# Q, K and V of two blocks at a time, and the second block's input ahead of the weights

## The chip, the cores and the metric

The kernel runs on the 8 cores of one Trainium2 chip, each core on one batch item of its own with nothing exchanged. The metric is the device time in microseconds (us) of the slowest core.

## The reference, cut to what matters

```python
def _L0_attn_ref(x, W_qkv, b_qkv, W_out, b_out):       # x: (8, 4096, 1024)
    qkv = x @ W_qkv + b_qkv
    q, k, v = jnp.split(qkv, 3, axis=-1)
    scores = jnp.einsum('bqd,bkd->bqk', q, k) / 32
    attn = jax.nn.softmax(scores, axis=-1)
    return jnp.einsum('bqk,bkd->bqd', attn, v) @ W_out + b_out

x = _layernorm(x + _L0_attn_ref(x, ...))
x = _layernorm(x + _L0_ffn_ref(x, controller, f1, f2, bias))   # 64 experts, arg-max routing in groups of 16 tokens
```

Only the first line of it, the projections to Q, K and V, is touched by the change.

## The kernel before, in words

Each core has x (4096 x 1024) and its transpose in float32. The program is five phases, one behind the other: the projections; attention with the output projection and the first layer norm; the router; the experts; and the combination with the second layer norm. Every engine has its own list of instructions, written by hand in program order with semaphore waits between them; nothing reorders them. All matmuls are issued at lines 129 and 132 (129 is the last of an accumulation, which counts a semaphore up), all DMAs at line 118, most work of ScalarE and VectorE at line 139.

The first phase has three kinds of transfers.

- Casting copies, float32 to bfloat16, all issued by POOL (GpSimd) in one burst and carried by one queue, q0: the transposed x in four pieces (columns 0 to 512, 512 to 1024, 1024 to 2048, 2048 to 4096) from DRAM to a DRAM scratch tensor `xbft`, each by `emit_xpiece`; the weights in 24 pieces of 128 x 1024 (8 for each of Q, K and V) into the tile `arenaA`; and at the end the whole of x into the scratch tensor `xbf` for use in the second phase.
- Loads, issued by SP (SyncE, queue q1): for each block of 512 columns eight copies of 128 x 512 from `xbft` into one of two buffers in `arenaA`. A load waits for its piece of `xbft` and for the last matmul that read the buffer (`xblk_T`).
- Stores, issued by ScalarE (queue q10): Q doesn't stay in SBUF. Each 128 x 512 result of Q is written by an activation into one of two slots of the tile `qstage`, and from there to the scratch tensor `qsp`. The activation waits until the store before last, from the same slot, has landed.

The work goes over 8 blocks of 512 columns. For each block TensorE makes 8 results of Q, 8 of K and 8 of V, each of 8 matmuls of 512 columns into one of the eight PSUM banks `pb`. Q and K take turns on banks 0 to 3 and are evicted by ScalarE, K into the tile `arenaB`; V takes turns on banks 4 to 7 and is evicted by VectorE into `arenaC`. Before a bank is written again TensorE waits for its last eviction (`bank_free`). The buffer of block b is given back at the end of V of block b, in line 273:

```python
        xblk_T[buf] = P_cnt["sT"]
```

and is loaded for block b+2 while block b+1 is computed. Then the second phase begins with SP's load of Q from `qsp`.

Of the kernel before, what the change touches and what calls it, by code (L numbers as in the profile page):

```python
# [10 lines left out]
AF = mybir.ActivationFunctionType  # L11
# [3 lines left out]
NCH = 8  # L15
# [6 lines left out]
def build_nc(S=4096, debug_scratch=False, stop_phase=99):  # L22
# [4 lines left out]
    NB = S // 512  # L27
# [26 lines left out]
    qsp_d = nc.dram_tensor("qsp", [NCH, 128, S], BF16, kind=SCR).ap()  # L54
# [9 lines left out]
    A = sb("arenaA", [128, 32768], BF16)  # L64
    B = sb("arenaB", [128, max(S * NCH, ISG_END)], BF16)
    C_ = sb("arenaC", [128, max(NT * 1024, NT * 512 + S + 512 + NT * 64 + QC + 4096 + 64)], BF16)
    FP = sb("arenaF", [128, 2048], F32)
    QS = sb("qstage", [128, 1024], BF16)
    BQ = sb("s_bqkv_pc", [128, 16], F32)
# [9 lines left out]
    pb = [es_.enter_context(nc.psum_tensor(f"pb{i}", [128, 512], F32))  # L79
          for i in range(8)]  # L80

    XB0 = 24576
# [25 lines left out]
    P_cnt = {s: 0 for s in CHANNELS + ["sT", "sV", "sC"]}  # L108
# [6 lines left out]
    def dma(eng, chan, dst, src, **kw):  # L115
        P_cnt[chan] += 16
        op(eng, lambda e, d=dst, s=src, kw=kw, sm=chan:
           e.dma_start(d, s, **kw).then_inc(sems[sm], 16))  # L118
        return P_cnt[chan]

    def wait(eng, sname, v):
        if v and v > 0:
            op(eng, lambda e, sm=sname, vv=v: e.wait_ge(sems[sm], vv))

    def t_mm(out, lhsT, rhs, start, stop, inc=False):
        if inc:
            P_cnt["sT"] += 1
            op("tensor", lambda e, o=out, l=lhsT, r=rhs, st=start, sp=stop:
               e.matmul(o, l, r, start=st, stop=sp).then_inc(sems["sT"], 1))  # L129
        else:  # L130
            op("tensor", lambda e, o=out, l=lhsT, r=rhs, st=start, sp=stop:
               e.matmul(o, l, r, start=st, stop=sp))  # L132
        return P_cnt["sT"]
# [13 lines left out]
    def c_op(method, *args, inc=False, **kw):  # L147
        return eng_op("scalar", "sC", method, *args, inc=inc, **kw)
# [27 lines left out]
    def emit_xpiece(i):  # L176
        if i < len(xpieces):
            lo, hi, ch = xpieces[i]
            dma("gpsimd", ch, xbft_d[:, lo:hi], xt_d[:, lo:hi])

    emit_xpiece(0)
    for pi, (koff, pref) in enumerate(((0, "wc"), (1024, "wck"), (2048, "wcv"))):
        for k in range(NCH):
            dma("gpsimd", "%s%d" % (pref, k),
                A[:, k * 3072 + koff: k * 3072 + koff + 1024],
                wqkv_d[k * 128:(k + 1) * 128, koff:koff + 1024])
        emit_xpiece(pi + 1)
    xbc_done = dma("gpsimd", "xbc", xbf_d[:, :], x_d[:, :])
    dma("sync", "sm", BQ[:], bqkv_pc_d)
    dma("sync", "sm", GLM[:], glmask_d)  # L190
# [2 lines left out]
    sm_done = dma("sync", "sm", FP[:, 0:1024], bv_t_d)  # L193
# [5 lines left out]
    bank_free = [("sV", 0)] * 8  # L199
    xblk_T = [0, 0]  # L200

    for b in range(NB):
        buf = b % 2
        xoff = XB0 + buf * 4096
        xchan = "xa%d" % buf
        wait("sync", xq_chan(b), 16)
        wait("sync", "sT", xblk_T[buf])
        xv = 0
        for c in range(NCH):
            xv = dma("sync", xchan, A[:, xoff + c * 512: xoff + (c + 1) * 512],  # L210
                     xbft_d[c * 128:(c + 1) * 128, b * 512:(b + 1) * 512])

        wait("tensor", xchan, xv)

        for kind in ("Q", "K"):
            koff = 0 if kind == "Q" else 1024
            for m in range(NCH):
                pbi = m % 4
                sem, val = bank_free[pbi]
                wait("tensor", sem, val)  # L220
                tv = 0
                for k in range(NCH):
                    if b == 0 and m == 0:
                        wait("tensor",
                             ("wc%d" if kind == "Q" else "wck%d") % k, 16)
                    lhsT = A[:, k * 3072 + koff + m * 128:
                             k * 3072 + koff + m * 128 + 128]
                    rhs = A[:, xoff + k * 512: xoff + (k + 1) * 512]
                    tv = t_mm(pb[pbi][:], lhsT, rhs, k == 0, k == NCH - 1,
                              inc=(k == NCH - 1))  # L230
                wait("scalar", "sT", tv)
                wait("scalar", "sm", sm_done)
                if kind == "Q":
                    slot = m % 2
                    qchan = "qs%d" % slot
                    wait("scalar", qchan, P_cnt[qchan])
                    qsl = QS[:, slot * 512: slot * 512 + 512]
                    cv = c_op("activation", qsl, pb[pbi][:], AF.Identity,
                              inc=True, bias=BQ[:, m:m + 1])
                    wait("scalar", "sC", cv)  # L240
                    dma("scalar", qchan, qsp_d[m, :, b * 512:(b + 1) * 512], qsl)
                else:
                    cv = c_op("activation",
                              B[:, m * S + b * 512: m * S + (b + 1) * 512],
                              pb[pbi][:], AF.Identity, inc=True,
                              bias=BQ[:, 8 + m:8 + m + 1])
                bank_free[pbi] = ("sC", cv)

        wait("vector", "sV", init_v)
        wait("vector", "sm", sm_done)  # L250
        for sub in range(4):
            tt = b * 4 + sub
            for half in range(2):
                pbi = 4 + (sub * 2 + half) % 4
                sem, val = bank_free[pbi]
                wait("tensor", sem, val)
                tv = 0
                for k in range(NCH):
                    if b == 0 and sub == 0 and half == 0:
                        wait("tensor", "wcv%d" % k, 16)  # L260
                    lhsT = A[:, xoff + k * 512 + sub * 128:
                             xoff + k * 512 + sub * 128 + 128]
                    rhs = A[:, k * 3072 + 2048 + half * 512:
                            k * 3072 + 2048 + (half + 1) * 512]
                    tv = t_mm(pb[pbi][:], lhsT, rhs, k == 0, k == NCH - 1,
                              inc=(k == NCH - 1))
                wait("vector", "sT", tv)
                vv = v_op("tensor_tensor",
                          C_[:, tt * 1024 + half * 512: tt * 1024 + (half + 1) * 512],
                          pb[pbi][:], FP[:, half * 512:(half + 1) * 512],  # L270
                          ALU.add, inc=True)
                bank_free[pbi] = ("sV", vv)
        xblk_T[buf] = P_cnt["sT"]

    qkv_T_done = P_cnt["sT"]
    if stop_phase <= 1:
# [45 lines left out]
    for qt in range(NQ):  # L322
# [4 lines left out]
        for pbi in (0, 1, 7):  # L327
            sem, val = bank_free[pbi]
# [5 lines left out]
        for sub in range(2):  # L334
            tt = qt * 2 + sub
            slot = tt % 2
# [29 lines left out]
        for kt in range(NKT):  # L366
# [5 lines left out]
            else:  # L372
                wait("scalar", "sT", sc_T[kt])
                if kt >= 4:
                    wait("scalar", "sT", kt_T[kt - 4])
                exp_v[kt] = c_op("activation", ebuf, pb[sp][:, 0:256], AF.Exp,
                                 inc=True, scale=1.0 / 32.0, bias=SM[:, 0:1])
# [10 lines left out]
            for c in range(NCH):  # L388
                pbi = 2 + c // 2
# [4 lines left out]
                lhsT = C_[:, kt * 1024 + c * 128: kt * 1024 + c * 128 + 128]  # L394
# [20 lines left out]
        for c in range(NCH):  # L415
            pbi = 2 + c // 2
# [195 lines left out]
    for qc in range(4):  # L612
        q0 = qc * QC
        base = (qc % 2) * QC
        for nb in range(QC // LGW):
            pbi = 6 + nb % 2
            sem, val = bank_free[pbi]
            wait("tensor", sem, val)
            wait("tensor", "cb", cbf_done)
            tv = 0  # L620
            for k in range(NCH):
                lhsT = C_[:, CBF + k * 64: CBF + (k + 1) * 64]
                if k < 3:
                    if k == 0 and nb == 0:
                        wait("tensor", "ha%d" % qc, P_cnt["ha%d" % qc])
                    rhs = A[:, HFA + k * S + q0 + nb * LGW:
                            HFA + k * S + q0 + (nb + 1) * LGW]
                else:
                    if qc == 0 and nb == 0:
                        wait("tensor", hfch[k], hf_done[k])  # L630
                    rhs = B[:, k * S + q0 + nb * LGW: k * S + q0 + (nb + 1) * LGW]
                tv = t_mm(pb[pbi][0:64, 0:LGW], lhsT, rhs, k == 0, k == NCH - 1,
                          inc=(k == NCH - 1))
# [35 lines left out]
    for ec in range(4):  # L669
# [4 lines left out]
        for t in range(NT):  # L674
            slot = t % 4
# [6 lines left out]
            tv = 0  # L682
            for c in range(NCH):
                pbi = b0 + c // 4
                qtr = c % 4
                if qtr == 0:
                    sem, val = bank_free[pbi]
                    wait("tensor", sem, val)
                lhsT = ht4(slot)[:, c * 128:(c + 1) * 128]
                rhs = C_[:, PB + t * 512 + ec * 128: PB + t * 512 + (ec + 1) * 128]  # L690
                tv = t_mm(pb[pbi][:, qtr * 128:(qtr + 1) * 128], lhsT, rhs,
                          qtr == 0, qtr == 3, inc=(c == NCH - 1))
# [83 lines left out]
        for esl in range(16):  # L776
            es = ec * 16 + esl
            slot = esl % 4
            if esl + 3 < 16:
                load_fw(esl + 3)  # L780
            cv = cv_cur
# [5 lines left out]
            for g0 in range(0, G, 128):  # L787
# [3 lines left out]
                for pbj in pb_pair:  # L791
                    sem, val = bank_free[pbj]
                    wait("tensor", sem, val)
                tv = 0
                for half in range(2):
                    pbj = pb_pair[half]
                    lhsT = B[0:64, INB + slot * 256 + g0:
                             INB + slot * 256 + g0 + gw]
                    rhs = B[0:64, F2B + slot * 1024 + half * 512:
                            F2B + slot * 1024 + (half + 1) * 512]  # L800
                    tv = t_mm(pb[pbj][0:gw, :], lhsT, rhs, True, True,
                              inc=(half == 1))
# [96 lines left out]
    for t in range(NT):  # L899
        slot = t % 5  # L900
# [7 lines left out]
        for half in range(2):  # L908
            sem, val = bank_free[b0 + half]
# [93 lines left out]
```

## Time and profile before

| what | value |
|---|---|
| runs shown | 2490.02 and 2619.9 us, median 2554.96 |
| the profiled execution | 2497.26 us |
| its span on the slowest core (core 0) | 2495.7 us |
| spans of the eight cores | 2457.5 to 2495.7 us |
| mean granted TensorE clock of the cores | 0.837 to 0.851 |
| TensorE busy, core 0 | 1962.3 us, 79% of the span |
| ScalarE, VectorE, POOL busy | 554.7, 516.7, 128.9 us |

The span goes from the first to the last instruction of a core; the device time of the profiled execution is 1.6 us more. Busy times overlap, so they don't add up to the span. All rows below are of core 0.

### The profile page before, as it was taken

How to read it: one execution, taken by the hardware profiler on the slowest of the kernel's cores; microseconds unless marked ns; L12 is line 12 of the kernel's file. 1: busy time of each engine (PE TensorE's matmuls, PEld its weight loads, DVE VectorE, ACT ScalarE, POOL GpSimd, SP SyncE). 2: the span in 40 equal slices, each digit the busy share in tenths (PEclk: the TensorE clock that was granted, in tenths of full speed). 3: DMA queues.
4: the chain of work that ended last, by engine and by line, in shares of the span. 5: the costliest groups of instructions: out<-in, count | busy, mean ns of one | idle time of the engine just before them, and what ended most of it. 6: DMA issues, size and time to landing. Idle time of an engine off the chain costs nothing.

```text
span 2495.7 us, 35949 instructions; the slowest of 8 cores (2457.5 to 2495.7 us)
## 1 busy us (share of the span) xinstructions
PE 1962.3 (79%) x13161; PEld 1309.2 (52%) x13216; DVE 516.7 (21%) x840; ACT 554.7 (22%) x1121; POOL 128.9 (5%) x242
## 2 busy tenths in 40 slices
PE   2624999989489999999999999995477676765554
PEld 0201444467467777887777778873243334332222
DVE  0000111101011111101111111011513333433555
ACT  0101222212112222222222222210063333432000
POOL 2000000010000000000000000000002011112110
PEclk9766999999799999999999999986655656555777
DMA  9995212089910100001000100003365656656996
GB/s 137 132 115 80 64 38 68 26 117 111 114 40 26 39 27 22 14 20 37 27 27 26 39 23 13 18 18 68 71 189 169 181 180 179 185 151 204 312 305 217
DMA packets 213271, 239.00 MB, mean 96 GB/s; under 512 B 113712, under 2 KB 148528, under 8 KB 212272
## 3 DMA queue, kind: packets, MB, share of 16 engines
q0 software_dynamic: 26080, 92.42, 20.2%
q1 hardware_dynamic: 92304, 85.54, 13.2%
q10 hardware_dynamic: 94720, 58.74, 8.2%
q8 instruction: 114, 1.87, 0.3%
q14 instruction: 53, 0.43, 0.1%
HBM read 203.22 MB, written 100.66 MB: 122 GB/s over the span
## 4 chain that ended last, share of the span: by engine, by line
PE 59%; DMA 23%; DVE 6%; another core or an unknown queue 4%; issue 4%; ACT 2%; SPq 1%; DVEq 1%; ACTq 0%; POOL 0%; POOLq 0%
PE pb L132 52%; PE pb L129 7%; DMA intersp<-arenaB 7%; DMA y<-arenaF 6%; DMA qsp<-qstage 4%; DMA arenaC<-hsp 3%; SPq L118 1%; DVE arenaF L141 1%; DVE arenaB L139 1%; DVEq L141 1%; DMA arenaA<-xbft 1%; DVE arenaA L139 1%; DMA arenaB<-f1b 1%; DMA xbft<-xt 1%
## 5 line engine op out<-in xcount | busy, mean ns | idle before, releaser
L132 PE MATMUL pb<-arenaA,arenaB 128*128 128x256 bf16 (+1 forms) x4032 | 587.4, 291 | 70.1 <-DMA arenaA<-qsp 45.6
L132 PE MATMUL pb<-arenaA 128*128 128x512 bf16 x1817 | 466.8, 392 | 161.2 <-ACT qstage L139 105.1
L132 PE MATMUL pb<-arenaA,arenaC 128*128 128x256 bf16 x4120 | 546.7, 277 | 25.9 <-DVE arenaA L139 18.5
L132 PEld LDWEIGHTS pb<-arenaA,arenaB 128*128 128x128 bf16 (+1 forms) x4032 | 417.6, 106 | 180.0 <-issue 123.5
L132 PEld LDWEIGHTS pb<-arenaA,arenaC 128*128 128x128 bf16 x4120 | 405.9, 99 | 84.1 <-issue 32.9
L139 ACT ACTIVATE arenaA<-pb,smalls 128x256 bf16<-128x256 f32 x512 | 240.7, 473 | 816.2 <-PE pb L129 784.8
L132 PEld LDWEIGHTS pb<-arenaA 128*128 128x128 bf16 x1856 | 181.9, 100 | 399.6 <-issue 219.2
L132 PE MATMUL pb<-arenaB 128*128 128x512 bf16 (+1 forms) x375 | 163.0, 523 | 151.0 <-DVE arenaB L139 66.3
L141 DVE RECIPROCAL arenaF<-pb 128x256 f32<-128x256 f32 x16 | 28.1, 1757 | 901.3 <-PE pb L129 901.3
L132 PEld LDWEIGHTS pb<-arenaB 128*128 128x128 bf16 (+1 forms) x384 | 40.8, 112 | 266.5 <-issue 255.2
L129 PE MATMUL pb<-arenaA,arenaB 128*128 128x256 bf16 (+1 forms) x576 | 167.3, 290 | 0.0
L139 DVE CAST arenaB<-pb 128x512 bf16<-128x512 f32 x128 | 88.5, 691 | 267.9 <-DMA intersp<-arenaB 177.2
L129 PE MATMUL pb<-arenaA,ones_t 128*128 128x256 bf16 x512 | 140.8, 275 | 0.0
L139 DVE TENSOR_TENSOR arenaC<-pb,arenaF 128x512 bf16<-128x512 f32 x64 | 44.2, 691 | 462.5 <-PE pb L129 462.5
L132 PE MATMUL pb<-arenaC 128*128 128x128 bf16 x896 | 99.5, 278 | 50.4 <-DMA arenaC<-hsp 33.4
L132 PEld LDWEIGHTS pb<-arenaC 128*128 128x128 bf16 x896 | 77.5, 126 | 71.6 <-issue 70.7
L139 ACT ACTIVATE arenaB<-pb 128x512 bf16<-128x512 f32 x128 | 75.7, 594 | 157.0 <-DMA intersp<-arenaB 152.5
L139 ACT ACTIVATE qstage<-pb,s_bqkv_pc 128x512 bf16<-128x512 f32 x64 | 44.0, 687 | 298.5 <-DMA qsp<-qstage 170.7
L141 DVE BATCH_NORM_STATS2 bnbuf<-pb 128x6 f32<-128x512 f32 x128 | 86.2, 694 | 115.2 <-PE pb L129 110.5
L118 POOL DMA_DIRECT2D intersp<-arenaB x128 | 69.2, 541 | 492.4 <-DVE arenaB L139 259.0
L141 ACT ACTIVATE bnbuf<-bnbuf,smalls 128x1 f32<-128x1 f32 x64 | 18.8, 294 | 335.6 <-DVE bnbuf L139 303.5
L139 ACT ACTIVATE arenaA<-pb 128x512 bf16<-128x512 f32 x128 | 76.2, 597 | 57.9 <-PE pb L129 57.2
(55 smaller groups left out, 946.4 us busy)
## 6 DMA issues: line engine op xcount, KB each, us to landing
arenaC<-hsp SPq DMA_DIRECT2D x128, 256.0 KB, 3.5
intersp<-arenaB POOLq DMA_DIRECT2D x128, 256.0 KB, 3.1
arenaB<-intersp SPq DMA_DIRECT2D x64, 256.0 KB, 17.7
arenaB<-intersp POOLq DMA_DIRECT2D x64, 256.0 KB, 9.3
y<-arenaF ACTq DMA_DIRECT2D x32, 512.0 KB, 10.1
xbf<-x POOLq DMA_DIRECT2D x1, 8192.0 KB, 209.1
arenaA<-xbft SPq DMA_DIRECT2D x64, 128.0 KB, 4.8
qsp<-qstage ACTq DMA_DIRECT2D x64, 128.0 KB, 2.0
```

The source lines that it names most:

```text
L118: e.dma_start(d, s, **kw).then_inc(sems[sm], 16))
L129: e.matmul(o, l, r, start=st, stop=sp).then_inc(sems["sT"], 1))
L132: e.matmul(o, l, r, start=st, stop=sp))
L139: getattr(e, m)(*a, **k).then_inc(sems[sname], 1))
L141: op(eng, lambda e, a=args, k=kw, m=method: getattr(e, m)(*a, **k))
```

## The change

The order of the casting copies: the second piece of the transposed x now stands right behind the first, ahead of all the weights, and the third and fourth stand behind all the weights. The order of the blocks: they are taken in pairs. Both loads of a pair are issued, then TensorE makes Q of the first and Q of the second block, then K of both, then V of both. The instructions within one block's Q, K or V are the same; they stand in functions now. Both buffers are given back at the end of the pair. S is 4096, so there are four pairs and the branch for a single block isn't used.

```diff
     emit_xpiece(0)
-    for pi, (koff, pref) in enumerate(((0, "wc"), (1024, "wck"), (2048, "wcv"))):
+    emit_xpiece(1)
+    for koff, pref in ((0, "wc"), (1024, "wck"), (2048, "wcv")):
         for k in range(NCH):
             dma("gpsimd", "%s%d" % (pref, k),
                 A[:, k * 3072 + koff: k * 3072 + koff + 1024],
                 wqkv_d[k * 128:(k + 1) * 128, koff:koff + 1024])
-        emit_xpiece(pi + 1)
+    emit_xpiece(2)
+    emit_xpiece(3)
     xbc_done = dma("gpsimd", "xbc", xbf_d[:, :], x_d[:, :])
...
-    for b in range(NB):
+    def load_xblk(b):
         buf = b % 2
...
-        wait("tensor", xchan, xv)
-
-        for kind in ("Q", "K"):
...
+        return xv
+
+    def qk_mms(b, kind):
+        xoff = XB0 + (b % 2) * 4096
+        koff = 0 if kind == "Q" else 1024
+        for m in range(NCH):
...
+    def v_mms(b):
+        xoff = XB0 + (b % 2) * 4096
...
-        xblk_T[buf] = P_cnt["sT"]
+
+    b = 0
+    while b < NB:
+        if b + 1 < NB:
+            xv0 = load_xblk(b)
+            xv1 = load_xblk(b + 1)
+            wait("tensor", "xa%d" % (b % 2), xv0)
+            qk_mms(b, "Q")
+            wait("tensor", "xa%d" % ((b + 1) % 2), xv1)
+            qk_mms(b + 1, "Q")
+            qk_mms(b, "K")
+            qk_mms(b + 1, "K")
+            v_mms(b)
+            v_mms(b + 1)
+            xblk_T[0] = P_cnt["sT"]
+            xblk_T[1] = P_cnt["sT"]
+            b += 2
...
```

The order on POOL at the start, as the difference (- before, + now); `xbft<-xt` are the pieces of the transposed x, `arenaA<-wqkv` the weights, `xbf<-x` the copy of x:

```order
 L157 UNCONDITIONAL_BRANCH
-L118 DMA xbft<-xt 1024x512
-L118 DMA arenaA<-wqkv 128x1024 x8
-L118 DMA xbft<-xt 1024x512
-L118 DMA arenaA<-wqkv 128x1024 x8
+L118 DMA xbft<-xt 1024x512 x2
+L118 DMA arenaA<-wqkv 128x1024 x24
 L118 DMA xbft<-xt 1024x1024
-L118 DMA arenaA<-wqkv 128x1024 x8
 L118 DMA xbft<-xt 1024x2048
 L118 DMA xbf<-x 256x16384
```

The 24 weight copies have become one run, with two pieces of x ahead of it and two behind.

On ScalarE, where Q of a block ends, before. `qstage` is Q's staging tile, `arenaB` holds K, qs0 and qs1 are the semaphores of the two slots:

```order
L139 ACTIVATE qstage<-pb,s_bqkv_pc 128x512 [waits sT,sm,qs1]
L118 DMA qsp<-qstage 128x512 [waits sC]
L139 ACTIVATE arenaB<-pb,s_bqkv_pc 128x512 [waits sT,sm] x8
L139 ACTIVATE qstage<-pb,s_bqkv_pc 128x512 [waits sT,sm,qs0]
L118 DMA qsp<-qstage 128x512 [waits sC]
```

And now, where Q of the second block of the pair ends:

```order
L139 ACTIVATE qstage<-pb,s_bqkv_pc 128x512 [waits sT,sm,qs1]
L118 DMA qsp<-qstage 128x512 [waits sC]
L139 ACTIVATE arenaB<-pb,s_bqkv_pc 128x512 [waits sT,sm] x16
L139 ACTIVATE qstage<-pb,s_bqkv_pc 128x512 [waits sT,sm,qs0]
L118 DMA qsp<-qstage 128x512 [waits sC]
```

Before, 8 activations with stores alternate with 8 without; now it is 16 with stores and then 16 without.

On TensorE, the seam behind the last result of Q of block 0, before (wck0 and wck1 are the semaphores of the first two pieces of K's weights):

```order
L132 MATMUL pb3<-arenaA 128x512 [waits sC]
L132 MATMUL pb3<-arenaA 128x512 x6
L129 MATMUL pb3<-arenaA 128x512
L132 MATMUL pb0<-arenaA 128x512 [waits sC,wck0]
L132 MATMUL pb0<-arenaA 128x512 [waits wck1]
```

And now (xa1 is the semaphore of the load of block 1):

```order
L132 MATMUL pb3<-arenaA 128x512 [waits sC]
L132 MATMUL pb3<-arenaA 128x512 x6
L129 MATMUL pb3<-arenaA 128x512
L132 MATMUL pb0<-arenaA 128x512 [waits xa1,sC]
L132 MATMUL pb0<-arenaA 128x512 x6
```

Behind Q of block 0 now comes Q of block 1, on the same bank, and the wait for K's weights has moved behind it. On SP the order of the instructions is the same as before; only the value of sT for which the loads of blocks 2, 4 and 6 wait is that of the end of the pair.

## Rows read from the trace of the kernel before

**Rows 1.** The page's slices (40 of 62.4 us): TensorE busy, DMA share, in tenths.

```profile
PE   2624999989489999999999999995477676765554
...
DMA  9995212089910100001000100003365656656996
```

**Rows 2.** TensorE's waits from 0 to 520 us: total, times, longest.

```profile
PE pb L132 <- ACT qstage L139: 105.1, 11, 44.9
PE pb L132 <- DMA arenaA<-xbft: 46.7, 1, 46.7
```

**Rows 3.** ScalarE in order of time: start, duration, what, idle before and releaser.

```profile
52.43 0.35 ACTq L118 DMA_DIRECT2D qsp<-qstage  x1
...
92.14 0.33 ACTq L118 DMA_DIRECT2D qsp<-qstage  x1
...
178.69 0.69 ACT L139 ACTIVATE qstage<-pb,s_bqkv_pc 128x512 bf16<-128x512 f32 x1 [50.08 <-DMA qsp<-qstage]
...
225.43 0.69 ACT L139 ACTIVATE qstage<-pb,s_bqkv_pc 128x512 bf16<-128x512 f32 x1 [11.43 <-DMA qsp<-qstage]
```

**Rows 4.** Stores: issued 92.1; 126.9; four from 226 to 235 with q10's records.

```profile
qsp<-qstage ACTq DMA_DIRECT2D x1, 128.0 KB, 16.5
...
qsp<-qstage ACTq DMA_DIRECT2D x1, 128.0 KB, 51.7
...
q10 hardware_dynamic: 588, 0.53, 17.5%
...
qsp<-qstage ACTq DMA_DIRECT2D x4, 128.0 KB, 1.9
```

**Rows 5.** DMA issues from 0 to 400 us: count, size, median us to landing.

```profile
xbf<-x POOLq DMA_DIRECT2D x1, 8192.0 KB, 209.1
...
xbft<-xt POOLq DMA_DIRECT2D x1, 4096.0 KB, 137.9
```

**Rows 6.** POOL's last issues; landing of x's first piece and the last V weights.

```profile
16.46 0.99 POOL L118 DMA_DIRECT2D xbft<-xt  x1
17.21 0.79 POOL L118 DMA_DIRECT2D xbf<-x  x1
...
xbft<-xt POOLq DMA_DIRECT2D x1, 1024.0 KB, 16.8
...
arenaA<-wqkv POOLq DMA_DIRECT2D x1, 256.0 KB, 94.2
```

**Rows 7.** Queues' records, MB, share: 92 to 108, 127 to 152, 160 to 210.

```profile
q10 hardware_dynamic: 287, 0.26, 6.0%
...
q0 software_dynamic: 384, 2.52, 95.3%
...
q10 hardware_dynamic: 203, 0.19, 2.2%
...
q0 software_dynamic: 157, 5.11, 94.4%
...
q10 hardware_dynamic: 126, 0.12, 0.7%
```

**Rows 8.** TensorE in order of time: the restart and the next phase's first matmuls.

```profile
226.26 3.14 PE L132 MATMUL pb<-arenaA 128*128 128x512 bf16 x7 [8.54 <-ACT qstage L139]
...
229.56 1.68 PE L132 MATMUL pb<-arenaA 128*128 128x512 bf16 x7
...
515.85 1.65 PE L132 MATMUL pb<-arenaA,arenaB 128*128 128x256 bf16 x7 [8.52 <-DMA arenaA<-qsp]
```

**Rows 9.** Stretches: busy us (and instructions) by engine, granted clock, DMA share, GB/s.

```profile
127.00:226.00 99.00, 14.54 (x51) 5.33 (x49) 0.00 (x0) 2.63 (x4) 0.00 (x0) 0.55 0.94 114
226.00:507.00 281.00, 276.68 (x1255) 125.34 (x1280) 38.02 (x55) 73.30 (x108) 0.00 (x0) 0.99 0.16 46
```

**Rows 10.** Loads of x issued at 383.5 and at 425.0, us to landing.

```profile
arenaA<-xbft SPq DMA_DIRECT2D x1, 128.0 KB, 4.9
...
arenaA<-xbft SPq DMA_DIRECT2D x1, 128.0 KB, 7.8
```

More of the change, by code:

```diff
@@ L211, in build_nc @@
                      xbft_d[c * 128:(c + 1) * 128, b * 512:(b + 1) * 512])
-        wait("tensor", xchan, xv)
-        for kind in ("Q", "K"):
[L216 to L247, printed above, removed]
@@ new lines, in load_xblk @@
+        return xv
[3 more added lines that the diff above has]
+        for m in range(NCH):
+            pbi = m % 4
+            sem, val = bank_free[pbi]
+            wait("tensor", sem, val)
+            tv = 0
+            for k in range(NCH):
+                if b == 0 and m == 0:
+                    wait("tensor",
+                         ("wc%d" if kind == "Q" else "wck%d") % k, 16)
+                lhsT = A[:, k * 3072 + koff + m * 128:
+                         k * 3072 + koff + m * 128 + 128]
+                rhs = A[:, xoff + k * 512: xoff + (k + 1) * 512]
+                tv = t_mm(pb[pbi][:], lhsT, rhs, k == 0, k == NCH - 1,
+                          inc=(k == NCH - 1))
+            wait("scalar", "sT", tv)
+            wait("scalar", "sm", sm_done)
+            if kind == "Q":
+                slot = m % 2
+                qchan = "qs%d" % slot
+                wait("scalar", qchan, P_cnt[qchan])
+                qsl = QS[:, slot * 512: slot * 512 + 512]
+                cv = c_op("activation", qsl, pb[pbi][:], AF.Identity,
+                          inc=True, bias=BQ[:, m:m + 1])
+                wait("scalar", "sC", cv)
+                dma("scalar", qchan, qsp_d[m, :, b * 512:(b + 1) * 512], qsl)
+            else:
+                cv = c_op("activation",
+                          B[:, m * S + b * 512: m * S + (b + 1) * 512],
+                          pb[pbi][:], AF.Identity, inc=True,
+                          bias=BQ[:, 8 + m:8 + m + 1])
+            bank_free[pbi] = ("sC", cv)
@@ L272, in build_nc @@
                 bank_free[pbi] = ("sV", vv)
-        xblk_T[buf] = P_cnt["sT"]
+    b = 0
[14 more added lines that the diff above has]
+            b += 2
+        else:
+            xv0 = load_xblk(b)
+            wait("tensor", "xa%d" % (b % 2), xv0)
+            qk_mms(b, "Q")
+            qk_mms(b, "K")
+            v_mms(b)
+            xblk_T[b % 2] = P_cnt["sT"]
+            b += 1
     qkv_T_done = P_cnt["sT"]
```

## The prediction

> **What bounds the kernel now.** A "group" below is eight matmuls into one PSUM bank; a block of 512 columns has 8 groups of Q, 8 of K and 8 of V, and the phase that the change touches has 192 groups. I read in this order: the page's slices, TensorE's waits, ScalarE in order of time, the DMA issues and queues by stretch, and TensorE in order of time.
>
> The slices show that for the first four of 40 (250 us) the DMA engines are full while TensorE is half idle, and that TensorE is then busy through slice 25 [rows 1]. TensorE's waits up to 520 us name who is late: 105.1 us in 11 waits on ScalarE's activations into the Q staging tile, and 46.7 us before the first matmul [rows 2]. ScalarE itself isn't slow: in order of time it stands idle before those activations, each time until a store of Q (qsp<-qstage) has landed. There are only two staging slots, so activation i of Q needs store i-2. The eight stores of block 0 take from 52.4 to 92.1+16.5 = 108.6 us; of block 1 the third activation waits 50.1 us, and the fifth starts only at 225.4, when the 11th store of all has landed [rows 3, 4].
>
> Why a store lasts so long stands in the queue views. POOL issues the casting copies in one burst, and their queue (q0) runs until the copy of x (8 MB) lands at 17.2+209.1 = 226.3 us; the last piece of x transposed lands at 16.5+137.9 = 154.4 [rows 5, 6]. A store issued in the quiet after that lands in 1.9 us and is 588/4 = 147 records of ACT's queue (q10). Beside q0, one issued at 92.1 took 16.5 us and one issued at 126.9 took 51.7 [rows 4]. ACT's queue moved 287 records in 16 us among the weights, 203 in 25 us mostly in the last piece of x transposed, and 126 in 50 us in the big copy [rows 7]. 
>
> At 226.3 us the stall ends. TensorE starts K of block 1, its 33rd group (the activation of 225.4 freed its bank), and runs with no gap to the end of the phase at 515.85-8.52 = 507.3 [rows 8, 9]: 160 groups in 281.0 us, 1.757 us each. So the phase's end is 226.3 plus the groups not yet done. That is what the change must be priced on.
>
> **The change part by part.** (1) POOL's queue: block 1's piece of x transposed goes ahead of the weights, and the 2 MB piece behind V's weights. No bytes are added, so the queue still ends at 226.3 and its last 4 MB piece still at 154.4. The 2 MB piece now takes the place where V's weights ended, 16.5+94.2 = 110.7 us [rows 5, 6]; from there on the records are big, as now. Q's weights come later by what the moved piece costs. The nearest row is piece 0, landed 16.8 us after issue [rows 6]: bounds 0 and 16.8. Much of it is hidden, for the load of block 0 keeps TensorE until 46.7 anyway. I take the first store at 55 instead of 52.4 (bounds 52 and 65). It costs nothing directly, only stores: 7 us is one store.
>
> (2) The order Q(0), Q(1), K(0), K(1), V(0), V(1). Before, eight stores stood in front of the first K, and 16 groups without any store (K and V of block 0) ran while stores drained. Now sixteen stores come in a row, and activations are in order, so nothing of K passes Q's last. Behind the waiting activation stand 16 activations of K on ScalarE; behind its bank all K and V on TensorE. How many stores land by 226.3? Up to 110.7 at the present pace, (108.6-52.4)/8 = 7.0 us: 55.7/7.0 = 8.0. To 154.4: 43.7/18.1 = 2.4. To 226.3: 71.9/58 = 1.2. Sum 11.6, so 12. The same sum for the kernel before (8, then 27.4/18.1, then 1.2) gives 10.7, and its 11th landed at 225.4 [rows 3], so it holds within a third of a store. With 12 landed, activations 1 to 14 are done and TensorE, four banks ahead, has done 18 groups, against 32 before. Cost: 14 groups x 1.757 = 24.6 us. Bounds: with a pace of 8.2 and a start at 65 the sum is 9.2 stores, 15 groups and +30; the other bound, that all are through in time, is rival A below, at 0.
>
> (3) The buffers' release. Both x buffers are now freed only by the last matmul of the pair, so blocks 2, 4 and 6 are loaded with TensorE empty. Before, each load ran beside a whole block. SP's 8 issues come again from the same line and the tensor queue waits for all of them. The nearest row is the end of this very phase: 1 MB in SP's queue after the last matmul, and TensorE is idle for 8.5 us [rows 8]. After a gap the first seven matmuls take 3.14 us where seven take 1.68 at full clock; the granted clock is 0.55 in 127 to 226 us, near the lower level of 1.2 GHz, and 0.99 after [rows 8, 9]: 1.5 more. So 10.0 us a boundary, three boundaries, 30 us. Bounds from loads that ran in this phase: one part of a load landed 4.9 us after its issue, and in another load 7.8 [rows 10]. If a single latency were all, 4.9+1.5; if the load is as slow as the second, 8.5+2.9+1.5; so 19 to 39 in all. Nothing hides it: only V's activations are still in flight there.
>
> (4) Reuse of weights: none. The same 3,452 rows of matmuls are issued, and each group loads its eight weight tiles again. So no gain here; I take 0. The phases behind 507 us only shift.
>
> The sum: profiled execution 2497.3 us (span 2495.7 and 1.6 around it) + 24.6 + 30.0 = 2551.9. The median of the runs shown, 2554.96, lies midway between runs of 2490.0 and 2619.9; my sum is against the profiled execution, which is near the lower, so the change would be 2.2% over its like.
>
> A rule on arbitration speaks against step (2). The trace's side: in the big copy ACT's queue got 126 records to q0's 157, so a store's nine records on an engine wait for about as many big ones [rows 7]. The Trainium skill, "DMA: Bandwidth & Descriptors", section "Queues, rings and completion order", says that an engine switches between rings only after a whole packet, typically some 9 to 17 descriptors. By that rule a store's share would go in one turn and the stores would be through early: this is rival A and its 2497, where this row gives 2552. By this row the trace disagrees, so I keep the row.
>
> **The rivals.** A: the stores get through. If the 14th lands by 154.4, the last activation of Q follows, and the other 29 groups of the pair (51.0 us) run to 206 us. The next load is then issued inside the big copy, where SP's loads of block 2 already waited; it lands some 6 us after 226.3; 144 groups x 1.757 = 253 and two boundaries of 10 give 505, to the phase's end of 507 now: 0, so 2497, not slower. It decides at a store every 7 us in all stretches. For it: that is the average pace up to 108.6. Against it: the store issued at 126.9, in the 4 MB piece, had not landed by 154.4 and needed 51.7 us [rows 4].
>
> B: partly through. The 14th lands at 190 in the middle of the big copy: 190 + 51 + 10 + 253 + 20 = 524, +17, so 2514. For it: engines don't run in step, and some get to the big records late. Against it: it needs two stores more than the rows give.
>
> C: a new wait inside each pair. Sixteen stores in a row now meet the load of the odd block in the queue; if a store takes 4.5 us instead of 1.9 for eight of them, each pair of blocks 2 to 7 loses some 13 us more: 2590. For it: those loads are one burst of 16 now. Against it: every block before also had a load beside its eight stores, and TensorE had no gap.
>
> D: the change doesn't do what it says, because TensorE keeps weights loaded between the two blocks. The order of rows excludes it.
>
> **How the numbers follow.** Forecast (12 or so stores by 226.3, three bare boundaries) 0.67, 2552, its own range 2536 to 2567. A 0.10 at 2497; B 0.13 at 2514; C 0.10 at 2590. About 2% is what a measurement of this kernel can tell from no change; 2% of 2497.3 is 50 us, so the line is at 2547. Two thirds of the forecast lies above it (0.46), and C: slower 0.56. The rest of it (0.21), B and most of A: within 2% 0.42. Faster 0.02, a part of A. The range from 2508 to 2595 leaves out A and little more.
>
> **What would show it right or wrong.** Right: a store of Q landing every 7 us up to 110 and hardly any from 155 to 226; TensorE's idle time up to 226 grown by about 24 us, and mostly put down to the Q staging activations; a first K group near 226; three new gaps of 8 to 9 us put down to arenaA<-xbft, and the phase's end near 562. Wrong: K groups before 160 us (A), a K group around 190 (B), gaps inside Q after 230 (C), or gaps at the pair boundaries under 5 us.

## The result

The changed kernel takes 2527.8 us (median of 9 runs) against 2488.3 us (median of 8) of the kernel before: a ratio of 1.0172, interval 1.0153 to 1.0190. Taken of 2488.3 us the ratio is 42.8 us; the two medians lie 39.6 us apart. Each ratio here compares only runs in which no half of the chip fell back to a lower clock, and of some kernels these are only two to four runs. The two runs of before that were shown ahead of the prediction had a median of 2554.96 because one of them was 2619.9; the profiled execution of 2497.3 us, against which I made the sum, was the nearer guide, though itself 9 us above the median of 2488.3.

### The profile after

TensorE's waits up to 570 us, on the slowest core (core 3), answer to [rows 2]. The columns are total, times, longest:

```profile
PE pb L132 <- ACT qstage L139: 113.7, 13, 40.5
PE pb L132 <- DMA arenaA<-xbft: 70.5, 4, 47.8
```

The wait on the staging activations has grown little (105.1 to 113.7 us). The wait on loads of x was one of 46.7 us and is now four of 70.5 in all. TensorE in order of time shows the three new ones, and the first matmul of the next phase, which was at 515.85 [rows 8]:

```profile
216.93 3.15 PE L132 MATMUL pb<-arenaA 128*128 128x512 bf16 x7 [20.22 <-ACT qstage L139]
...
276.73 3.15 PE L132 MATMUL pb<-arenaA 128*128 128x512 bf16 x7 [7.71 <-DMA arenaA<-xbft]
...
369.50 3.15 PE L132 MATMUL pb<-arenaA 128*128 128x512 bf16 x7 [7.05 <-DMA arenaA<-xbft]
...
462.83 3.15 PE L132 MATMUL pb<-arenaA 128*128 128x512 bf16 x7 [7.93 <-DMA arenaA<-xbft]
...
554.06 1.65 PE L132 MATMUL pb<-arenaA,arenaB 128*128 128x256 bf16 x7 [6.40 <-DMA arenaA<-qsp]
```

The three boundaries cost 7.7, 7.1 and 7.9 us of idle time, and each restarts at the lower clock of 1.2 GHz (3.15 us for seven matmuls where seven take 1.67 later; the granted clock is 0.50 of full speed from 276.7 to 280 us). The phase ends at 554.06 - 6.40 = 547.7 us; I had it near 562. The last stall inside Q is over at 216.9 us, 9 us sooner than I had placed it. ScalarE in order of time says why, beside [rows 3]:

```profile
130.71 0.69 ACT L139 ACTIVATE qstage<-pb,s_bqkv_pc 128x512 bf16<-128x512 f32 x1 [8.63 <-DMA qsp<-qstage]
...
148.34 0.69 ACT L139 ACTIVATE qstage<-pb,s_bqkv_pc 128x512 bf16<-128x512 f32 x1 [16.95 <-DMA qsp<-qstage]
...
192.30 0.69 ACT L139 ACTIVATE qstage<-pb,s_bqkv_pc 128x512 bf16<-128x512 f32 x1 [43.27 <-DMA qsp<-qstage]
...
216.10 0.69 ACT L139 ACTIVATE qstage<-pb,s_bqkv_pc 128x512 bf16<-128x512 f32 x1 [23.11 <-DMA qsp<-qstage]
```

These are activations 13 to 16 of Q; the last one means that the 14th store has landed. I had counted 12 stores by 226; the 15th, issued at 193.1, landed 29.8 us later, at 222.9. The queues' records from 127 to 152 us, and then from 160 to 210 us, stand against [rows 7]:

```profile
q0 software_dynamic: 363, 2.71, 103.5%
q10 hardware_dynamic: 288, 0.26, 8.0%
...
q0 software_dynamic: 162, 5.31, 98.2%
q10 hardware_dynamic: 161, 0.15, 1.1%
```

ACT's queue moved 288 and 161 records where it had moved 203 and 126.

One more stretch counts, 110 to 127 us. The kernel before has no store on its way there, so that it gave no price for it; the changed kernel has (all queues together, the copy queue, ACT's queue):

```profile
DMA packets 732, 1.95 MB, mean 115 GB/s; under 512 B 32, under 2 KB 330, under 8 KB 732
...
q0 software_dynamic: 402, 1.65, 94.6%
q10 hardware_dynamic: 330, 0.31, 6.7%
```

The 4 MB piece of the transposed x is being moved there (the 2 MB piece had landed 90.7 us after its issue, at about 107), every record is under 8 KB, those of the copy queue have 4.1 KB on average, and ACT's queue gets 330 records in 17 us: a store costs 147/19.4 = 7.6 us, no more than beside the weights. From 127 to 152 us, in the kernel before, it is otherwise:

```profile
DMA packets 889, 3.01 MB, mean 120 GB/s; under 512 B 59, under 2 KB 518, under 8 KB 853
```

36 of the records are over 8 KB there, one of them an instruction fetch. The other 35 can only be the big copy's, of 32 KB, on DMA engines that are through with the 4 MB piece already; they carry 1.1 of the copy queue's 2.52 MB. So that stretch was a mixture and not the 4 MB piece.

In the table below, the phase's end is the start of the second phase's first matmul less TensorE's idle time before it, as a mean over the eight cores of one profiled execution; before this was 506.8 and after 543.2 us. The jobs ran on several chips, on which the kernel before had medians of 2463 to 2488 us, so ratios are taken within a job.

| kernel | phase's end, us | ratio to before (95% interval) |
|---|---|---|
| the changed kernel | 543.2 | 1.0172 (1.0153 to 1.0190) |
| changed, old order of the copies | 539.0 | 1.0142 (1.0061 to 1.0223) |
| before, new order of the copies | 496.3 | 0.9961 (0.9928 to 0.9995) |
| changed, early release | 511.7 | 1.0056 (1.0017 to 1.0096) |
| changed, small records | 498.7 | 1.0013 (0.9977 to 1.0049) |
| changed, copy in halves | 508.4 | 1.0070 (1.0044 to 1.0096) |
| before, small records | 464.6 | 0.9855 (0.9828 to 0.9883) |
| changed, early release and small records | 470.5 | 0.9871 (0.9833 to 0.9909) |
| before, load of block 2 behind the copy | 499.1 | 0.9989 (0.9974 to 1.0004) |
| changed, early release, copy by pair | 446.0 | 0.9776 (0.9751 to 0.9801) |
| before, copy by block | 429.4 | 0.9739 (0.9703 to 0.9775) |
| before, copy by block, last x pieces late | 409.8 | 0.9632 (0.9604 to 0.9660) |

What lies behind the phase's end hardly differs within a job of experiments: from the first matmul of the second phase to the end of the span it is 1944 to 1949 us in the first four experiments, as a mean over the cores. So the phase's end carries the verdicts there. Between the profiles of before and after themselves it doesn't: the same stretch is 1970 us before and 1956 after, so the ends of the phase are 36.4 us apart and the device times 42.8. A phase's end comes from one execution, over whose cores it scatters by 4 to 27 us; differences under some 5 us are not settled by it.

### The profile page after: what moved, and what is told of

Its sections match the earlier page's. It is cut to its first block, busy times and chain, and to the rows that moved or that the text cites. A ratio compares the mean times of both kernels' runs of the same rounds, so it can differ in the third digit from the quotient of the medians.

```text
span 2525.2 us, 36004 instructions; the slowest of 8 cores (2482.0 to 2525.2 us)
## 1 busy us (share of the span) xinstructions
PE 1960.5 (78%) x13216; PEld 1299.6 (51%) x13216; DVE 516.5 (20%) x840; ACT 554.6 (22%) x1121; POOL 128.9 (5%) x242
## 4 chain that ended last, share of the span: by engine, by line
PE 60%; DMA 23%; DVE 5%; another core or an unknown queue 4%; issue 3%; ACT 2%; SPq 2%; DVEq 1%; ACTq 0%; POOL 0%; POOLq 0%
PE pb L132 52%; PE pb L129 7%; DMA intersp<-arenaB 7%; DMA y<-arenaF 5%; DMA arenaC<-hsp 4%; DMA qsp<-qstage 4%; SPq L118 2%; DMA arenaA<-xbft 1%; DVE arenaB L139 1%; DMA arenaB<-f1b 1%; ACT arenaB L139 1%; DMA xbft<-xt 1%; DVE bnbuf L141 1%; DVE arenaA L139 1%
## 5 line engine op out<-in xcount | busy, mean ns | idle before, releaser
L132 PE MATMUL pb<-arenaA 128*128 128x512 bf16 x1856 | 482.5, 397 | 186.7 <-ACT qstage L139 113.7
L132 PE MATMUL pb<-arenaA,arenaC 128*128 128x256 bf16 x4120 | 540.7, 275 | 26.0 <-DVE arenaA L139 18.9
```

## The experiments

### Which part of the change costs: the order of the copies

The changed kernel with the order of POOL's copies as it was before:

```diff
     emit_xpiece(0)
-    emit_xpiece(1)
-    for koff, pref in ((0, "wc"), (1024, "wck"), (2048, "wcv")):
+    for pi, (koff, pref) in enumerate(((0, "wc"), (1024, "wck"), (2048, "wcv"))):
...
-    emit_xpiece(2)
-    emit_xpiece(3)
+        emit_xpiece(pi + 1)
```

> The changed kernel with the order of the casting copies of before (weights of Q first, then the second piece of the transposed x, and so on); pairs of blocks stay. Theory: the loss is all in the order of the blocks, namely some 15 us because 16 stores of Q in a row drain through the busy copy queue, and some 27 us in three gaps at the pair boundaries. The copies' order is neutral: ratio to before 1.017, within 0.004, three gaps of 7 to 8 us on arenaA<-xbft still there. Rival: the second piece of x ahead of Q's weights delays the start and costs part of the loss; then the ratio falls to 1.012 or less.

And the reverse, the kernel before with the new order of the copies:

> The kernel before with only the new order of the casting copies. Theory: neutral, since Q of block 0 is paced by its stores until 90 us and the queue ends at the same time: ratio 1.000, within 0.003, and TensorE still restarts near 226 us. Rival: the order itself costs: ratio 1.004 or more; or it helps, since V's weights land 20 us earlier: 0.996 or less.

Measured: 1.0142 with an interval that holds 1.017, phase's end 539.0; and 0.9961, phase's end 496.3. The pairs with the old order of copies keep the loss, and the new order alone doesn't make one; at most it gains 0.4%, just outside what I allowed for. Whether it gains at all is open: the medians of the two kernels in that job, 2460.0 and 2463.4 us, are only 0.14% apart. Without the early piece of x, a wait of 14.6 us appears inside the first pair, for the load of block 1; it replaces in part time that was spent waiting for stores:

```profile
84.76 3.15 PE L132 MATMUL pb<-arenaA 128*128 128x512 bf16 x7 [14.58 <-DMA arenaA<-xbft]
```

### The boundaries: early release

```diff
             v_mms(b)
-            v_mms(b + 1)
             xblk_T[0] = P_cnt["sT"]
+            v_mms(b + 1)
             xblk_T[1] = P_cnt["sT"]
```

> The changed kernel, but the first block's buffer of a pair is given back at the end of its own V instead of at the end of the pair, so that the load of the next pair runs beside V of the second block (8 groups, 14 us). Theory: the three gaps of 7.7, 7.1 and 7.9 us and their half-clock restarts of 1.5 us go, 27 us in all; what is left is the longer stall: ratio 1.006, within 0.003; the phase ends near 520 instead of 547.7 us. Rival: the load isn't hidden, or only the first part; the gaps shrink by less than half and the ratio stays at 1.012 or more.

Measured: 1.0056, phase's end 511.7 against 539.0 of the other pair kernel in the job: 27.3 us. That kernel has the old order of copies, so the two differ in this as well; but the three gaps read above, 22.7 us, and three restarts of 1.5 us give the same 27.2. Of TensorE's waits for loads of x this kernel has that for block 0 left and no other:

```profile
PE pb L132 <- DMA arenaA<-xbft: 46.3, 1, 46.3
```

So the release at the pair's end costs 27 us, and 511.7 - 496.3 = 15.4 us are left for the stall of the stores. The ratios leave 14 us against the kernel before (0.0056) and 23 against the same kernel with the new order of copies (1.0056 - 0.9961 = 0.0095), so its size is known only roughly.

### The stall: the size of a record

```diff
-    xbc_done = dma("gpsimd", "xbc", xbf_d[:, :], x_d[:, :])
+    for h in range(2):
+        xbc_done = dma("gpsimd", "xbc", xbf_d[:, h * 512:(h + 1) * 512],
+                       x_d[:, h * 512:(h + 1) * 512])
```

> The changed kernel, but the copy of x (8 MB) is issued as two copies of 512 columns each, so that its records are 1 KB instead of 32 KB; same bytes, same place in the queue. Theory: the size of a record of the copy queue sets how long a store waits, since an engine takes about one of a store's 9 records for each one or two of that queue. Stores of Q then land every 7 to 11 us throughout, the 14th by about 155 us instead of 216; K and V of the pair run to about 205, and the load of block 2 takes 10 to 20 us in the still busy queue: the phase ends near 495 and the ratio is 0.995, within 0.006. Rival: the bytes decide, since the DMA engines are full either way; then the last waits of 40 and 20 us on qstage stay and the ratio is 1.017.

Measured: 1.0013, phase's end 498.7. ScalarE in order of time has the 14th store landed at 148.9 us, not at 216:

```profile
148.86 0.69 ACT L139 ACTIVATE qstage<-pb,s_bqkv_pc 128x512 bf16<-128x512 f32 x1 [6.60 <-DMA qsp<-qstage]
```

TensorE in order of time restarts there for good, and the load of block 2 now waits 22 us in the busy queue:

```profile
149.69 3.15 PE L132 MATMUL pb<-arenaA 128*128 128x512 bf16 x7 [3.72 <-ACT qstage L139]
...
224.35 3.15 PE L132 MATMUL pb<-arenaA 128*128 128x512 bf16 x7 [22.25 <-DMA arenaA<-xbft]
```

The copy queue from 160 to 210 us moves the same bytes in 5170 records as it did in 162:

```profile
q0 software_dynamic: 5170, 5.28, 99.1%
```

The DMA engines are as full as before and the stores pass, so it isn't the bytes. What changes is the size of a record and with it the piece of memory that one covers; these two were not taken apart. The mechanism and the phase's end (495 expected) came out; the ratio did not (0.995 expected), since I had started from 507 us as the end before, and on this chip it is probably near 496, that of the kernel before with the new order of copies.

The same edit in the kernel before:

> The kernel before (one block at a time) with the copy of x issued as two copies of 512 columns, records of 1 KB. Theory: the stall of Q of block 1 from 127 to 226 us is the big records; with small ones the stores and the load of block 2 get through within 10 to 30 us, TensorE goes on from about 150 and the phase ends near 430 to 445 instead of 496: ratio 0.977, within 0.006. Rival: the full DMA engines hold it up whatever the records' size: 0.99 or more.

Measured: 0.9855, phase's end 464.6, some 25 us later than expected. The stall of 99 us is gone, but stores in the small-record stretch still land only every 7 to 10 us (block 1's, over the cores), and TensorE still waits 59.5 us for them, 44 of these in Q of blocks 1 and 2. The theory is right in kind, and it promised too much. Small records bring back the pace that stores have beside the weights and beside records of 4 KB (7.0 and 7.6 us each), and not more. The counts of records, 160 to 190 us, on the slowest core:

```profile
q0 software_dynamic: 2983, 3.04, 96.9%
q10 hardware_dynamic: 563, 0.51, 7.6%
```

Here five of the copy's records go for one of a store's. "One for one or two", from which I had reasoned, holds beside records of 4 and of 32 KB alone; what sets the pace beside small records stays open.

### Both repairs in the pair form

> The changed kernel with both repairs: records of 1 KB in the copy of x, and the first buffer of a pair given back after its own V. Theory: TensorE has 20 of 192 groups done at 149 us and then runs without a gap but for the load of block 2, which starts at about 188 inside the copy and takes up to 22 us, of which 14 are covered: phase end 149 + 172 x 1.73 + 10 = 457, ratio 0.984, within 0.005; so the pairs stay behind the single blocks with the same records. Rival: pairs are as good as single blocks once both faults are gone: ratio within 0.003 of that of the single blocks with small records.

Measured: 0.9871, within the 0.005 of the theory and also within 0.003 of the single blocks' 0.9855, so the ratio doesn't decide. The phase's end is 470.5, 13 us later than the theory's 457; pairs are 6 us behind by it, in one execution of each.

### Moving the copy out of the way

First the changed kernel with the copy in halves:

```diff
             qk_mms(b + 1, "Q")
+            if b < 4:
+                wait("gpsimd", "sT", P_cnt["sT"])
+                xbc_done = dma("gpsimd", "xbc", xbf_d[b * 1024:(b + 2) * 1024, :],
+                               x_d[b * 1024:(b + 2) * 1024, :])
             qk_mms(b, "K")
```

> The changed kernel, but the copy of x is issued in two halves, each behind the last matmul of Q of pair 0 and of pair 1, where TensorE does K and V and nothing is stored or loaded for some 55 us; its records stay at 32 KB. Theory: the stores of Q no longer meet the big records; the 14th lands by about 155 us, the pair's K and V run to 207, the first half (36 us) ends before the load of block 2; three boundary gaps of 7 to 8 us stay: phase end near 490 on this chip (539 with the copy in place) and ratio 0.998, within 0.006, a little better than with small records in place, where the load of block 2 still met the copy and waited 22 us. Rival: copies cost the same wherever they stand, or the second half, beside pair 1, stalls the stores and loads there: ratio 1.005 or more.

Measured: 1.0070, phase's end 508.4: a miss. POOL in order of time shows what I overlooked:

```profile
120.88 0.52 POOL L118 DMA_DIRECT2D xbf<-x  x1 [103.39 <-PE pb L129]
```

And TensorE in order of time, what it led to:

```profile
171.03 2.29 PE L132 MATMUL pb<-arenaA 128*128 128x512 bf16 x5 [35.94 <-ACT qstage L139]
```

TensorE runs four banks ahead of ScalarE, so its last matmul of Q is done at 120.9 us with six stores still to land, and the half copy goes ahead of those. The wait of 36 us ends at 171, where I had expected the 14th store to be through by 155. The gaps at the boundaries were 8.4, 8.3 and 8.7 us.

Then the kernel before with the copy cut by block:

```diff
+        wait("gpsimd", "sT", P_cnt["sT"] - 6)      # the second result of K is done
+        xbc_done = dma("gpsimd", "xbc", xbf_d[b * 512:(b + 1) * 512, :],
+                       x_d[b * 512:(b + 1) * 512, :])
```

> The kernel before, with the copy of x cut into eight pieces of 512 rows, each issued when TensorE is at the third result of K of its block, so that it runs (9 us) beside K and V, where nothing is stored. Records stay big. Theory: the stall at 127 to 226 us goes but for what the 4 MB piece of the transposed x costs up to 154; TensorE goes on from about 155 at the latest: phase end near 440, ratio 0.977, within 0.006. Rival: the later pieces delay each block's load or stores, and half of it is given back: 0.988 or more.

Measured: 0.9739, phase's end 429.4, 10 us better than expected. TensorE's waits on staging are 32.3 us in 5 instead of 105.1 in 11. The last two of them, in order of time:

```profile
142.15 3.15 PE L132 MATMUL pb<-arenaA 128*128 128x512 bf16 x7 [8.33 <-ACT qstage L139]
...
151.75 3.14 PE L132 MATMUL pb<-arenaA 128*128 128x512 bf16 x7 [6.03 <-ACT qstage L139]
```

The last stall ends at 151.8 us, some 3 us behind the landing of the 4 MB piece of the transposed x. Its pair form, with early release:

> The changed kernel with the first buffer given back after its own V, and with the copy of x in pieces of 512 rows, two beside the K of each pair, so that from 154 us on no big record meets a store and no boundary is bare. It is the pair form of the kernel with copies by block (phase end 429 us, ratio 0.974). Theory: what pairing itself costs is left: at about 155 us, when the queue runs dry, TensorE has done 20 groups, against 30 to 34 of the single blocks, since 16 stores stand ahead of the first K: phase end 155 + 172 x 1.73 = 453, ratio 0.983, within 0.005, and some 20 us behind the single blocks. Rival: pairing costs nothing once the queue is out of the way: ratio 0.974, within 0.004.

Measured: 0.9776 (0.9751 to 0.9801), phase's end 446.0; 7 us better than the theory had it, inside the rival's range and 0.0004 outside the theory's. It was on another chip than the single blocks, with TensorE's first matmul at 48.9 us instead of 46.2, so of the 17 us between the two phase's ends about 14 are left for pairing. That pairs are behind is likely, and not settled by the ratios.

Last, the single blocks with the last pieces of the transposed x moved too:

```diff
-    xb_bounds = sorted(set(min(v, S) for v in (0, 512, 1024, 2048, S)))
+    xb_bounds = sorted(set(min(v, S) for v in (0, 512, 1024, 2048, 3072, S)))
...
-        emit_xpiece(pi + 1)
...
+        if pi < 2:
+            emit_xpiece(pi + 1)
...
+        if b in (1, 3):
+            emit_xpiece(3 + b // 2)
```

> The kernel before with the copies of x by block, and with the 4 MB piece of the transposed x cut into two pieces of 1024 columns, issued beside K of blocks 1 and 3. Theory: the queue of the start then ends with V's weights at about 92 us, so V of block 0 starts some 15 us earlier, and the stores of block 1 land in 2 us each: TensorE has 16 groups done by 92 us and doesn't wait again: phase end 92 + 176 x 1.73 = 397 plus 5 for late pieces, ratio 0.963, within 0.006. Rival: the start is bound by the weights' bytes and later pieces collide with loads: 0.972 or more, as with the copies of x by block alone.

Measured: 0.9632 (0.9604 to 0.9660) as expected, 2392.9 us against 2482.6; the phase's end is 409.8 where the theory had 402. This is the best version: it beats the kernel before by 3.7% and, by the ratio of the ratios of two jobs (0.9632/1.0172), the changed one by 5.3%. TensorE's waits on staging are down to 26.4 us in 9.

From 100 us on it is busy for 309.5 of 315 us, at a granted clock of 1.00 (the busy times by engine, the clock, the DMA share and GB/s of that stretch):

```profile
100.00:415.00 315.00, 309.50 (x1431) 139.37 (x1428) 44.72 (x65) 79.06 (x116) 5.64 (x10) 1.00 0.47 86
```

### Why the stores were quicker than priced

> The kernel before, but SP issues the load of block 2 only when the copy of x has landed (the load itself, 1 MB, is needed only at Q of block 2 and takes 9 us in quiet). Theory for the stores being quicker in the changed kernel than I priced them: there SP's queue held nothing in that stretch; here it holds 72 records per engine, which take turns with the stores. Without them ACT's queue moves 160 to 260 records from 160 to 210 us instead of 126 to 145, the 11th store lands by 218 instead of 225, TensorE restarts by 219 and the phase ends 5 to 8 us earlier: ratio 0.997, within 0.003. Rival: the turn goes by the big records alone and the longer burst of stores was the reason: 126 to 145 records again, restart at 222 to 226, ratio 1.000.

Measured: 0.9989 (0.9974 to 1.0004), phase's end 499.1, which tells neither from the other by time. The 11th store lets its activation start at 219.7 us as a mean over the cores, against 224.1 before; the big copy lands sooner too, so this doesn't decide either. ACT's queue tells more. In the big copy, 160 to 210 us, on the slowest core:

```profile
q10 hardware_dynamic: 167, 0.15, 1.1%
```

As a mean over the eight cores these are 167 records without SP's load beside them, 138 in the kernel before and 153 in the changed one. So SP's queue did take some of the turns there. In 127 to 152 us the means are 205 without the load and 195 with it, against 283 in the changed kernel: there the load is not the reason. The start of the burst is a part of it. In the kernel before, whose first store of block 1 was issued at 126.9 us, ACT's queue has no record at all from 127 to 131 us and these in the next two stretches of 5 us (131 to 136, 136 to 141):

```profile
q10 hardware_dynamic: 46, 0.05, 2.7%
...
q10 hardware_dynamic: 77, 0.07, 4.1%
```

In the changed kernel, whose stores run all the time, it has 76 records from 127 to 131 on the slowest core. As means over the cores the first 4 us have 12 records before and 62 in the changed kernel, the other 21 us have 183 and 221. So the start accounts for 50 of the 88 records that I missed in this stretch; where the other 38 come from stays open.

## Why the prediction was right or wrong

The mechanism was right in its parts, and the size was off by 12 us: +54.6 forecast, +42.8 measured. 2552 was a ratio of 1.0219 to the profiled execution, and 1.0172 came. In absolute time 2552 is 24 us over the 2527.8 measured, and 9 of these are the start from a profiled execution above its median. The time lies in the range of 2508 to 2595, but below the line of 2% on whose other side I had put 0.56.

- **Step (1), the order of the copies: right.** No cost shows (1.0142 without it, in an interval of 1.0061 to 1.0223; 0.9961 alone). The first store went out at 53.5 us, between the 52.4 of before and my 55.
- **Step (2), sixteen stores in a row: the mechanism right, the term mis-sized.** I had 24.6 us; the experiments leave 15.4 by the phase's end, 14 to 23 by the ratios. The step that failed is the price of a store from 110.7 us on: 18.1 us in the 4 MB piece and 58 in the big copy. The sum reads 8.0 + 2.4 + 1.2 stores. Up to 110 us the count was exact: 8 had landed. From there to 154 I had 2.4, and 4 landed (core 3: 115, 121, 131, 148 us); then the 13th and 14th landed at 192 and 216 and ended the stall, where I had 1.2 up to 226.
- **Where the price went wrong.** With the changed kernel's own records, as means over the cores, the sum comes out. From 110.7 to 127 us its ACT queue moved 19.3 records a us, 2.1 stores, where I had 0.9 (16.3/18.1). From 127 to 154.4 it moved 11.3 a us, again 2.1 stores, where I had 1.5. From 154.4 to 226.3 it moved 3.1 a us, 1.5 stores, where I had 1.2. Together with the 8 that is 13.7, and the 14th ended the stall. So more than half of what I missed lies ahead of 127 us. My row for "the 4 MB piece" was 127 to 152 us, in which the engines that were ahead moved the big copy's records of 32 KB already; beside the piece's own 4 KB records a store cost 7.6 us and not 18.1. "From there on the records are big", from 110.7, was the false reading. The smaller parts are the start of the burst inside that window, and in the big copy the turns that SP's load of block 2 took, which the pair form doesn't issue there.
- **The groups.** From core 3 they can be counted: 269.0 - 216.9 = 52.1 us from the last stall to the first boundary, less 1.5 for the restart, is 28.8 groups of 1.757 us, so 19.2 were done at 216.9 and 23.7 at 226.3, where I had 18, against 32 before. 8.3 groups x 1.757 = 14.6 us.
- **Step (3), the buffers' release: right.** 30.0 us forecast, 27.3 measured. The wait is 7.1 to 7.9 us and not 8.5; the restart costs the 1.5 us I gave it.
- **Step (4), no reuse of weights: nothing that contradicts it** in the rate of 1.73 to 1.76 us a group, before and after. The "3,452 rows" named there stand in no row shown; this phase has 192 groups of eight matmuls, 1536.
- **The rivals.** A has the 14th store at 154.4 us and B at 190; it landed at 197 to 221 us over the cores, so B was the nearer of the two, and a part of its gain is what the sum had too much. C, a new wait inside the later pairs, isn't there: the last wait for staging in the changed kernel is the one that ends at 216.9 us. D is excluded as said.
- **The signs.** Two were ill chosen. The first K group, the 17th, starts at 131.7 us on core 3, which I had named a sign of A; but with TensorE four banks ahead my own 12 stores would have let two K groups through before 226 as well. And TensorE's idle time up to 226 was to grow by some 24 us. It grew from 153.9 to 161.5. In the 64.8 us in which it was busy the changed kernel did 23.7 groups, the kernel before 32 in 72.3: it waited before nearly every group, and seven matmuls behind such a wait mostly took 3.1 us instead of 1.7, so this part of the stall isn't idle time.
- **The rule on arbitration.** I had set one store record for one or two of the copy's records against the Trainium skill's whole packets of some 9 to 17 descriptors ("DMA: Bandwidth & Descriptors", section "Queues, rings and completion order"). In the big copy of the changed kernel the counts are 161 to 162, one for one, and a record of the copy takes 0.982 x 16 x 50/162 = 4.85 us of an engine. If a store's nine records on an engine went in one turn, a store would be through after one or two of these, in 5 to 10 us; the 13th and 14th took 60.7 and 66.9 us from issue to landing. So the trace disagrees, provided that a record of the profile is what the page calls a descriptor, which no run here shows. One for one is not general either: beside records of 1 KB it was five of the copy's for one.

## What to carry to other kernels

When small transfers wait behind a bulk copy, look at the size of the copy's records and not only at its bytes. Here a store of 128 KB cost some 7 to 10 us beside records of 1 and of 4 KB, and 46 us beside records of 32 KB (147/3.2). Cut the records, or better, issue the copy piece by piece where nobody else needs the queues. Reordering work so that its stores bunch up makes this worse, and a double buffer that is given back in pairs is no longer a double buffer. And price a wait from a stretch in which it is in full swing and in which only one kind of record passes: a window that holds the start of a burst, or in which some engines have gone on to the next transfer, makes it too dear.

## What the runs showed that I had not expected

- Cutting the copy's records from 32 KB to 1 KB didn't slow it: 5.28 MB in 5170 records in 50 us, against 5.31 MB in 162.
- A wait of POOL for TensorE's last matmul of Q releases at 120.9 us, six stores too early; with four banks between them TensorE's count says little about the stores.
- A burst of stores into the busy engines moves nothing at first: issued at 126.9 us, no record by 131. In the changed kernel, where another store was always on its way, ACT's queue had 76 records in those 4 us.
- The DMA engines don't work in step: while some were still at the 4 MB piece, others moved the big copy's records.
